# Five experts' weights scaled and split on GpSimd instead of VectorE, with ScalarE's roundings at other steps

## The reference

```python
    nx = _rmsnorm(X, g2)
    xf = nx.reshape(-1, d)
    logits = xf @ Wr.T + expert_bias
    rw = jax.nn.softmax(logits, axis=-1)
    topw, topi = jax.lax.top_k(rw, TOP_K)
    topw = jax.nn.softmax(topw, axis=-1)
    combine = jnp.sum(jax.nn.one_hot(topi, NUM_EXPERTS, dtype=xf.dtype) * topw[..., None], axis=1)
    shared = _swiglu(xf, sW1, sW2, sW3)
    h = jax.nn.silu(jnp.einsum('td,efd->etf', xf, eW1)) * jnp.einsum('td,efd->etf', xf, eW3)
    eo = jnp.einsum('etf,edf->etd', h, eW2)
    specialist = jnp.einsum('te,etd->td', combine, eo)
    moe_out = (shared + specialist).reshape(B, S, d)
    return X + moe_out
```

## Time and profile before

| | us |
|---|---|
| runs of the kernel before, median of 3 | 1522.15 |
| their lowest and highest | 1520.98, 1525.44 |
| span of the profiled execution, first to last instruction | 1465.9 |
| busy: TensorE matmul | 1342.3 |
| busy: VectorE | 1123.4 |
| busy: ScalarE | 892.0 |
| busy: GpSimd | 793.0 |

### The profile page before, as it was taken

One profiled execution on the slowest core, in us unless ns is written; L12 is line 12 of the kernel. 1 busy time (PEld: TensorE's weight loads), 2 busy tenths in 40 slices (PEclk: granted clock), 3 DMA queues, 4 the chain that ended last, 5 costly groups with the idle time before them and its releaser, 6 DMA issues.

```text
span 1465.9 us, 43550 instructions
## 1 busy us (share of the span) xinstructions
PE 1342.3 (92%) x15663; PEld 1176.4 (80%) x15664; DVE 1123.4 (77%) x2225; ACT 892.0 (61%) x2229; POOL 793.0 (54%) x836
## 2 busy tenths in 40 slices
PE   4799999999889999889999999878998888999993
PEld 4788988888679999778888888667886667888882
DVE  4798888888845565789999999878885797554557
ACT  3567767776556666646566665557775545555556
POOL 2556656665535454456555564578884005777740
PEclk9799999999999999989999999999997999999996
DMA  8200000000130000000000000010003203333318
GB/s 227 53 7 8 10 8 8 8 10 9 34 81 5 1 0 0 3 9 8 9 9 8 10 7 9 27 53 15 14 14 117 94 2 119 103 101 98 97 41 341
DMA packets 79895, 65.09 MB, mean 44 GB/s; under 512 B 48878, under 2 KB 73457, under 8 KB 78706
## 3 DMA queue, kind: packets, MB, share of 16 engines
q1 hardware_dynamic: 72818, 44.98, 10.6%
q0 software_dynamic: 6912, 17.84, 3.9%
HBM read 39.18 MB, written 18.35 MB: 39 GB/s over the span
## 4 chain that ended last, share of the span: by engine, by line
PE 77%; DVE 10%; issue 5%; ACT 4%; POOL 2%; DMA 1%; SPq 0%; DVEq 0%; ACTq 0%; POOLq 0%
PE psQ L1957 13%; PE psW L2050 12%; PE psQ L2352 8%; PE psW L2331 5%; PE psS L2075 4%; PE psS L2024 4%; PE psT L1986 3%; PE psQ L2153 3%; PE psS L2153 3%; PE psW L2141 3%; PE psM L2141 3%; PE psM L2011 3%; PE psT L2320 1%; PE psM L1975 1%; PE psT L2339 1%
## 5 line engine op out<-in xcount | busy, mean ns | idle before, releaser
L742 POOL TENSOR_TENSOR pn<-ex,rden 128x1024 f32<-128x1024 f32 x64 | 143.8, 2247 | 234.1 <-PE psT L1986 211.7
L1957 PEld LDWEIGHTS psQ<-xT,wq 128*128 128x128 f32 x1536 | 202.8, 202 | 46.3 <-issue 24.2
L1957 PE MATMUL psQ<-xT,wq 128*128 128x256 f32 x1536 | 222.9, 299 | 1.7 <-ACT cur L1067 1.5
L2050 PE MATMUL psW<-wout,oT 128*128 128x256 f32 x1536 | 208.2, 291 | 7.0 <-ACT oT L976 4.8
L2050 PEld LDWEIGHTS psW<-wout,oT 128*128 128x128 f32 x1536 | 193.2, 192 | 13.2 <-ACT oT L976 7.5
L2352 PE MATMUL psQ<-W,exT 128*128 (+1 forms) x624 | 172.6, 412 | 0.0
L782 POOL TENSOR_TENSOR hT<-hf,hT 128x512 fp32r<-128x512 f32 x64 | 85.8, 1340 | 99.4 <-ACT hT L1063 99.2
L862 POOL DMA_INDIRECT rows<-xf,src x72 | 73.1, 1016 | 108.7 <-DVE src L1839 83.4
L2352 PEld LDWEIGHTS psQ<-W,exT 128*128 128x128 f32 x624 | 111.3, 192 | 18.9
L2331 PE MATMUL psW<-W,ehT 128*128 (+1 forms) x624 | 102.7, 301 | 8.3 <-DVE ehT L1869 8.2
L925 ACT ACTIVATE qT<-psQ 128x512 f32<-128x512 f32 x128 | 76.6, 598 | 52.9 <-PE psQ L1957 50.9
(11 more groups left out here) (313 smaller groups left out, 3474.2 us busy)
## 6 DMA issues: line engine op xcount, KB each, us to landing
both<-results SPq DMA_DIRECT2D x8, 1024.0 KB, 12.6
raw_w<-W SPq DMA_DIRECT2D x27, 256.0 KB, 4.1
vv<-vp SPq DMA_DIRECT2D x256, 16.0 KB, 1.8
xf<-xf_all SPq DMA_DIRECT2D x4, 1024.0 KB
out<-X SPq DMA_DIRECT2D x8, 512.0 KB, 5.1
X<-x SPq DMA_DIRECT2D x1, 3584.0 KB, 18.1
bvv<-v_all SPq DMA_DIRECT2D x128, 16.0 KB, 1.8
rows<-xf,src POOLq DMA_INDIRECT x72
```

The costliest lines, as they stand in the source:

```text
L742: nc.gpsimd.tensor_tensor(pn[:], ex[t % 2][:, :, 0:S], rden[:].unsqueeze(2).to_broadcast([P, H, S]), ALU.mult).then_inc(sem("t_pn"), 1)
L1957: mm = nc.tensor.matmul(psQ[:, cc, h * QT:h * QT + QT], wq[w][:, k, c * P:c * P + P], xT[g % 2][u][:, k, :], start=(k == 0 and j == 0), st ...
L2050: mm = nc.tensor.matmul(psW[:, 0:D], oT[u][:, c, :], wout[w][:, c, :], start=(u == 0 and c == 0 and w == 0), stop=(u == 1 and c == CH - 1))
```

## The change

GpSimd takes over experts 1 to 5 (`POOL_SPLITS`). It first multiplies `g2col` into the raw weights in place (`scale_expert`: two TENSOR_SCALAR 128x512 an expert, signal `e_scaled`), in the order 1, 2, then later 3, 4, and 5; between these it makes the low halves (`split_lo`: three TENSOR_TENSOR 128x512 an expert, signal `e_plo`), each behind its own scaling and ScalarE's rounding. ScalarE rounds the scaled weights with scale 1.0 and waits for `e_scaled` before parts 0 and 1. The steps of its pieces move: of expert 1 from 0, 1, 2 to 1, 1, 2; of expert 3 from 10, 10, 10 to 10, 10, 11; of expert 4 from 19 to 11, 12, 12; of expert 5 from 20 to 13, 13, 15. VectorE keeps only experts 0, 6, 7 and 8. The loads' semaphore `e_last` becomes a further count of `e_rest`, and two semaphores of the first stage are merged into one.

```diff
-SPLIT_STEP = ([-4, -3, -2] + [0, 1, 2] + [3, 4, 5] + [10, 10, 10] + [SLOTS] * 3 + [TABLES] * 3 + [21] * 3 + [22] * 3 + [23] * 3)
+SPLIT_STEP = ([-4, -3, -2] + [1, 1, 2] + [3, 4, 5] + [10, 10, 11] + [11, 12, 12] + [13, 13, 15] + [21] * 3 + [22] * 3 + [23] * 3)
+
+POOL_SPLITS = range(1, 6)
...
@@ SyncE
-                load_expert(p, p + 1, sem("e_last"))
+                load_expert(p, p + 1, sem("e_rest"))
@@ GpSimd, behind its block pipeline
+            def scale_expert(n):
+
+                pool.wait_ge(*((sem("e_first"), 2 * 48) if n == 1 else (sem("e_first"), 3 * 48) if n == 2 else (sem("e_rest"), 3 * 48)))
+                for part in range(KD):
+                    raw = raw_w[:, ORDER[n], 1, part * 2 * D:part * 2 * D + 2 * D]
+                    nc.gpsimd.tensor_scalar(raw, raw, g2col[:, part:part + 1], None, ALU.mult).then_inc(sem("e_scaled"), 1)
+
+            def split_lo(n):
+
+                for part in range(3):
+                    third = slice(part * 2 * D, part * 2 * D + 2 * D)
+                    if part < KD:
+                        pool.wait_ge(sem("e_scaled"), KD * POOL_SPLITS.index(n) + part + 1)
+                    pool.wait_ge(sem("e_whi"), 3 * n + part + 1)
+                    nc.gpsimd.tensor_tensor(W[:, ORDER[n], 1, third], raw_w[:, ORDER[n], 1, third], W[:, ORDER[n], 0, third].bitcast(F32),
+                                            ALU.subtract).then_inc(sem("e_plo"), 1)
+
+            scale_expert(1)
+            scale_expert(2)
+            split_lo(1)
+            split_lo(2)
+            scale_expert(3)
+            scale_expert(4)
+            split_lo(3)
+            scale_expert(5)
+            split_lo(4)
+            split_lo(5)
@@ ScalarE, split_expert
-                elif (n, part) == (5, 0):
-                    act.wait_ge(sem("e_rest"), 3 * 48)
                 elif (n, part) == (6, 0):
-                    act.wait_ge(sem("e_last"), 3 * 48)
+                    act.wait_ge(sem("e_rest"), 2 * 3 * 48)
+                by_pool = n in POOL_SPLITS
+                if by_pool and part < KD:
+                    act.wait_ge(sem("e_scaled"), KD * POOL_SPLITS.index(n) + part + 1)
...
-                                     scale=g2col[:, part:part + 1] if part < KD else 1.0).then_inc(sem("e_whi"), 1)
+                                     scale=1.0 if by_pool or part == KD else g2col[:, part:part + 1]).then_inc(sem("e_whi"), 1)
@@ VectorE, first_half
-                    if SPLIT_STEP[piece] == i:
+                    if SPLIT_STEP[piece] == i and piece // 3 not in POOL_SPLITS:
                         split_expert(piece // 3, piece % 3)
@@ TensorE, expert_step
-                        pe.wait_ge(sem("e_wlo"), 3 * EP if t else 3)
+                        pe.wait_ge(sem("e_wlo"), 3 * (EP - len(POOL_SPLITS)) if t else 3)
+                        if t:
+                            pe.wait_ge(sem("e_plo"), 3 * len(POOL_SPLITS))
```

More of the change, by code:

```diff
@@ L521, in load_layer @@
                     sp.dma_start(first_q[:], a[L["wq"]].rearrange("(k p) n -> p k n", p=P)).then_inc(sem("f_loaded"), 16)
-                    sp.dma_start(r_small[:], a["r_small"]).then_inc(sem("rel_loaded"), 16)
+                    sp.dma_start(r_small[:], a["r_small"]).then_inc(sem("rel_moved"), 16)
                     sp.dma_start(raw_kvn[:, :, 0:2 * DH], a[L["wkv"]].rearrange("(k p) n -> p k n", p=P)).then_inc(ld, 16)
@@ L586, in _ @@
             sp.wait_ge(sem("rel_turn"), 5 + REL["out"])
-            sp.dma_start(rel_dram, r_out[:].unsqueeze(1).to_broadcast([H, S, P])).then_inc(sem("rel_stored"), 16)
-            sp.wait_ge(sem("rel_stored"), 16)
+            sp.dma_start(rel_dram, r_out[:].unsqueeze(1).to_broadcast([H, S, P])).then_inc(sem("rel_moved"), 16)
+            sp.wait_ge(sem("rel_moved"), 32)
             sp.dma_start(bias_t[0:S, :, :], bass.AP(rel_dram.tensor, S - 1, [[P - 1, S], [S * P, H], [1, S]])).then_inc(sem("l_braw"), 16)
@@ L1458, in _ @@
                 norm_lo(0, t)
-            dve.wait_ge(sem("rel_loaded"), 16)
+            dve.wait_ge(sem("rel_moved"), 16)
             nc.vector.scalar_tensor_tensor(r_h[:], r_rows["w0"][:], r_pos[:, 0:1], r_rows["b0"][:], ALU.mult,
```

## The result

Ten runs of each kernel give 1529.91 us (median) for the changed kernel and 1523.37 us for the kernel before. The ratio is 1.0048, with a 95% interval of 1.0034 to 1.0063: 5.2 to 9.6 us slower (the medians are 6.54 us apart). The forecast was 1528.1 us, +5.95 us.

The account below looks back on a forecast made before the run. VectorE sets the pace between 1151.7 and 1182 us; later everything waits for the last experts' loads. 0 + 1.0 - 1.15 + 0.35 + 5.25 + 0.5 + 0 = +5.95 us on 1522.15 gives 1528.1 us, range 1521.0 to 1532.0.

Parts of the forecast that it names:

- Steps 19 and 20, experts 4 and 5: VectorE's pieces there cost 3.86 us, but removing them gains 0: VectorE then waits some 2 us for the last loads.
- Step 10: Expert 3's three pieces leave VectorE, so `eh` of the next step starts earlier: 1.15 us gained.
- Step 1: ScalarE's rounding of expert 1 waits for two GpSimd scalings, taken as 0.65 us each: costs nothing.
- Step 7: GpSimd's four scalings of experts 3 and 4 run into the two-input VectorE instructions of `choose(0)`: +1.0 us.
- the waiting one pays the whole of the other: VectorE and GpSimd alternate; in an unbroken row a GpSimd instruction costs its duration less 0.36: scaling 0.29, subtraction 0.93 us.
- Step 11: Six GpSimd instructions hold up VectorE's COPY and TENSOR_TENSOR pairs: +5.25 us, plus 0.35 for `ehT` waiting on TensorE.
- Step 13: Of expert 5's first two subtractions, one stands in the way of VectorE's first two-input instruction: +0.5 us.
- What lies around the span: The profiled span, 1465.9 us, is 56.25 less than the runs' median; what lies around it was taken as untouched.
- COPY is not held: Rival: GpSimd does not hold VectorE's COPY in the scan; +4.0 us, 1526.15 us. Chance 0.20.
- A scaling costs as much as a subtraction: Rival: a scaling takes 1.29 us, costing more at steps 1, 7 and 11; +10.65 us, 1532.8 us. Chance 0.15.
- GpSimd is not in the way: Rival: GpSimd's instructions fall into VectorE's PSUM heads of the steps, leaving only the 1.15 us gain; 1521.0 us. Chance 0.15.
- The load is not last: Rival: removing the pieces of steps 19 and 20 does shorten the path by 3.86 us; 1517.1 us. Chance 0.04.

Follow-up runs that it names:

- experiments 1 and 2: 1: the change without GpSimd work in the routing, ratio 1.0034. 2: three last-load waits for one, in that kernel (1.0024) and the kernel before (1.0019).
- experiment 4: The change without its ten GpSimd scalings, its 15 subtractions kept and ScalarE rounding unscaled weights: ratio 1.0032 to the kernel before, routing stretch 89.26 us.
- the placed kernel: Against before: GpSimd has only experts 3 to 5, each instruction held until VectorE's PSUM operations; last loads awaited per expert. Ratios 0.9967 and 0.9980.

## Why the prediction was right, point by point

The sign, the size (+5.95 forecast, +6.54 between medians) and the place of the loss were right. Several terms were not, and they made up for each other: step 1 came out 1.95 us dearer than the sum had it, steps 11 to 13 1.2 us cheaper. That the total is so close is in part luck. Against before's first trace:

- **Steps 19 and 20, experts 4 and 5: 0.** Measured -2.14, and +2.02 in step 21: -0.12; the wait there became 2.24 us, for "some 2". Right, and shown by experiments 1 and 2. The reason given was half of it; time in which TensorE keeps VectorE waiting hid the other half.
- **Step 10: -1.15.** Measured -1.16. Right.
- **Step 1: 0.** Measured +1.5, and +0.45 more up to step 7 (in which an `xf` takes 1.36 us beside a subtraction). The scalings alone give +1.48 up to step 7 and the subtractions alone nothing (21.28 and 19.79 in the table), so the 0.45 needs both. Wrong, by the size of a scaling: 0.65 us was taken, worked out from the select's ns per element. The select works on 1024 elements of 64 partitions at 0.95 ns an element; the scaling takes 2.5. The working chose 0.65 between a bound of 1.29 and one from the select (1144 ns for 1024 elements, so some 0.57 for 512), because "the number of inputs is what differs most", and the true price lies beyond both. The rival with 1.29 us had the mechanism, and +1.2 for this place.
- **Step 7: +1.0.** Measured +0.75, and +0.38 in step 8, where nothing was put: 1.13 together. Nearly right, by two errors: the scalings are longer (1.57) but each holds at most 0.38, and one of the four holds nothing. The rule "the waiting one pays the whole of the other", drawn from selects and two-input instructions, does not hold for a scaling.
- **Step 11: +5.6.** Measured +2.40 there and +2.50 in step 12, where nothing was put: 4.90 together. COPY is held, as taken. Fewer subtractions fell into the scan, since the two longer scalings pushed them back into the tile ends. Of the 4.90, TensorE's wait has 0.39 (put at 0.35), the two scalings 1.08 (put at 0.9), and four subtractions 3.44, or 0.93, 0.88, 0.51 and 1.12 (put at 4.3: 0.85 and three times 1.15). The general price of a subtraction in an unbroken row, 0.93, was right (0.95 in experiment 4), but the sum did not use it for these three.
- **Step 13: +0.5.** Measured 0; the first two subtractions of expert 5 met the tile ends of step 12 and PSUM instructions.
- **What lies around the span: 56.25 us.** Wrong. The changed kernel's profiled run took 1523.63 us with a span of 1521.8. The gap lies in the routed loop, which took 54 us less in the profiled execution of before than in that of the change, and isn't time around a span. Nothing of the sum rested on it.

Sum of the measured steps: -0.12 - 1.16 + 1.95 + 1.13 + 4.90 + 0.14 (steps 13 to 18) = 6.84.

The signs. Of what the prediction said would show it, the start of the last nine loads is as told: 6.96 us later in the stretch (81.36 and 74.40 us behind the last root) for about 6. The others are not. A scaling takes 1.57 us and not 0.65; one `upto` row takes over 1 us, the other held ones 0.54 to 0.63; step 11 takes 6.70 us and not 10, as half the cost lies in step 12; `xff` is 1.5 us later; and ScalarE's wait for the loads is 5.83 us, not longer than 5.96. The number was better than the picture behind it.

The rivals. *COPY is not held* fell: 1.10 us. *A scaling costs as much as a subtraction* was right on the length at step 1 and wrong on the hold; it would have given +10.65. *GpSimd is not in the way* fell for this order, and is what the placed kernel makes true. *The load is not last* fell with experiment 1.

## What to carry to other kernels

Work moved to an idle engine costs what it holds up, not what it takes: ask of each instruction of the other engine beside it whether the two hold each other, and put it where they don't; and ask who now waits for its result (ScalarE at step 1, 1.5 us). Here the same fifteen instructions cost 6.3 us right behind their data and nothing at the heads of the steps, with one wait each. And a relief in front of a transfer is worth something only together with the edit that lets the transfer's first part be used: apart, the two gave 0.5 and 0.2 us, together 2.3.
